# Another order of matmuls around the border batches, and four stores issued by GpSimd, in a two-layer convolution kernel

## The reference

```python
def _gn(v, G=32, eps=1e-05): ...            # per image and channel: (v - mean) / sqrt(var + eps)

x = x + _L0_conv_ref(_gn(x), w3, b3, w5, b5, wr, br)
x = x + _L1_conv_ref(_gn(x), filters)
```

```python
feat = (spot[..., :, None] * spot[..., None, :]).reshape(spot.shape[:-1] + (M * M,))
out = jnp.einsum('bcyxf,ocf->boyx', feat, filters.reshape(O, C, M * M))
```

## Time and profile before

| | |
|---|---|
| median of 3 runs | 304.87 us (304.46 to 305.16) |
| profiled execution | 305.6 us, span from first to last instruction 303.9 us |
| mean granted TensorE clock | 0.979 |
| TensorE matmul busy | 276.0 us, 91%, 6464 multiplies |
| VectorE busy | 251.5 us, 83% |
| ScalarE busy | 88.1 us, 29% |
| GpSimd busy | 33.0 us, 11% |
| DMA | 11.45 MB |

### The profile page before, as it was taken

One profiled execution on the slowest core, in us unless ns is written; L12 is line 12 of the kernel. 1 busy time (PEld: TensorE's weight loads), 2 busy tenths in 40 slices (PEclk: granted clock), 3 DMA queues, 4 the chain that ended last, 5 costly groups with the idle time before them and its releaser, 6 DMA issues.

```text
span 303.9 us, 13566 instructions
## 1 busy us (share of the span) xinstructions
PE 276.0 (91%) x6464; PEld 125.6 (41%) x6464; DVE 251.5 (83%) x216; ACT 88.1 (29%) x135; POOL 33.0 (11%) x82
## 2 busy tenths in 40 slices
PE   0579999899999999999999999999999999999930
PEld 0124443343334434436457455333334446447310
DVE  1899899995999999599999999976999999950330
ACT  5432016949258989529000000004000000000000
POOL 7913970000110000000000000000000000000000
PEclk9999999979999999999999999999999999999985
DMA  6973000000000000000000000085000000000049
GB/s 191 382 193 82 4 3 2 2 5 2 2 2 4 4 2 2 4 2 5 2 2 4 4 2 4 2 172 111 2 2 4 2 2 4 2 4 4 2 86 190
DMA packets 19206, 11.45 MB, mean 38 GB/s; under 512 B 17744, under 2 KB 17872, under 8 KB 19024
## 3 DMA queue, kind: packets, MB, share of 16 engines
q1 hardware_dynamic: 14640, 9.06, 11.7%
q10 hardware_dynamic: 4512, 1.53, 2.2%
HBM read 6.40 MB, written 4.19 MB: 35 GB/s over the span
## 4 chain that ended last, share of the span: by engine, by line
PE 80%; DVE 7%; ACT 3%; issue 3%; DMA 2%; SPq 1%; DVEq 0%
PE acc L1007 63%; PE acc L1050 15%; ACT raw L507 3%; DMA raw<-in_x 2%; DVE stats L741 2%; PE acc L1101 2%; DVE plane L759 1%; DVE raw L801 1%; DVE arena L669 1%; ACT arena L497 1%; DVE scaled L637 0%; DVE norm L756 0%; SPq L314 0%; SPq L321 0%; DVE mean_var L746 0%
## 5 line engine op out<-in xcount | busy, mean ns | idle before, releaser
L1007 PE MATMUL acc<-product,weight 32*32 32x512 f32 (+1 forms) x3040 | 128.6, 605 | 0.0
L1007 PEld LDWEIGHTS acc<-product,weight 32*32 32x32 f32 (+1 forms) x3040 | 61.7, 110 | 63.8 <-issue 51.1
L879 DVE TENSOR_TENSOR product<-plane 128x4096 f32<-128x4096 f32 x19 | 83.3, 4427 | 0.1
L1007 PE MATMUL acc<-raw,weight 32*32 32x512 f32 (+1 forms) x992 | 44.3, 605 | 0.0
L1050 PE MATMUL acc<-product,middle 32*64 32x512 f32 (+1 forms) x576 | 30.6, 621 | 0.0
L1007 PEld LDWEIGHTS acc<-raw,weight 32*32 32x32 f32 (+1 forms) x992 | 20.4, 111 | 20.7 <-issue 16.2
L801 DVE TENSOR_TENSOR raw<-acc,arena 128x512 f32<-128x512 f32 x16 | 9.9, 684 | 18.9 <-issue 18.7
L741 DVE BATCH_NORM_STATS2 stats<-raw 128x6 f32<-128x512 f32 x32 | 19.7, 686 | 3.1 <-DMA raw<-in_x 3.1
L879 DVE TENSOR_TENSOR raw<-plane 128x4096 f32<-128x4096 f32 x5 | 22.2, 4433 | 0.0
L1007 PE MATMUL acc<-product,arena 32*32 32x512 f32 (+1 forms) x448 | 22.0, 606 | 0.0
L507 ACT ACTIVATE raw<-arena 32x512 f32<-32x512 f32 x32 | 21.9, 683 | 0.5
(11 more groups left out here) (121 smaller groups left out, 213.9 us busy)
## 6 DMA issues: line engine op xcount, KB each, us to landing
raw<-in_x SPq DMA_DIRECT2D x8, 512.0 KB, 8.5
out<-raw SPq DMA_DIRECT2D x24, 128.0 KB, 2.9
arena<-in_L_conv_filters SPq DMA_DIRECT2D x4, 400.0 KB, 6.9
out<-raw ACTq DMA_DIRECT2D x8, 128.0 KB, 4.6
arena<-in_L_conv_w ACTq DMA_DIRECT2D x4, 100.0 KB, 4.0
w_in<-in_L_conv_w ACTq DMA_DIRECT2D x2, 36.0 KB, 1.9
w_in<-in_L_conv_w SPq DMA_DIRECT2D x2, 36.0 KB, 2.1
b_in<-in_L_conv_b SPq DMA_DIRECT2D x2, 0.5 KB
```

The lines of the kernel that those rows point to most:

```text
L879: nc.vector.tensor_tensor(both_halves(g, u), plane_halves(g), plane_halves(g, PRODUCTS[k][0] * PITCH + PRODUCTS[k][1]), ALU.mult)\
L1007: return nc.tensor.matmul(acc[32 * s:32 * (s + strips), j, r, :], weights[32 * r:32 * r + 32, t:t + strips, :] .rearrange("p t c -> p (t c ...
```

## The change

Group two's "total" is issued as two rounds of pairs, the border columns, two more rounds of pairs and then the round of singles; before, the singles stood between the two border batches and all four rounds of pairs behind. The rest of the first layer for group two begins with singles. In the second layer's first unit of g = 0, singles and pairs change places, so that the pairs stand between the border batches. Of group two's 16 stores, GpSimd issues strip 2 of every image with a semaphore of its own; SP issues strip 0 of every image and strip 3 of images 1 and 3, ScalarE's queue strip 1 and strip 3 of images 0 and 2.

```diff
+        stored_by_pool = sem("stored_by_pool")
...
-        def store(eng, g, r, strips):
+        def store(eng, g, r, strips, done):
...
-                              .rearrange("p (y x) -> p y x", x=W)).then_inc(stored, 16)
+                              .rearrange("p (y x) -> p y x", x=W)).then_inc(done, 16)
+
+        def store_last(eng, strips, parity, done):
+
+            for r in range(GROUP):
+                eng.wait_ge(evicted, 3 * GROUP + r + 1)
+                store(eng, 1, r, strips + ((3,) if r % 2 == parity else ()), done)
...
-                store(sp, 0, r, range(STRIPS))
-            for r in range(GROUP):
-                sp.wait_ge(evicted, 3 * GROUP + r + 1)
-                store(sp, 1, r, (0, 1))
-            sp.wait_ge(stored, 16 * NG * GROUP * STRIPS)
+                store(sp, 0, r, range(STRIPS), stored)
+            store_last(sp, (0,), 1, stored)
+            sp.wait_ge(stored, 16 * (NG * GROUP * STRIPS - GROUP))
+            sp.wait_ge(stored_by_pool, 16 * GROUP)
...
             stream_borders(raw[1]).then_inc(borders, 1)
+            store_last(pool, (2,), None, stored_by_pool)
...
-            for r in range(GROUP):
-                act.wait_ge(evicted, 3 * GROUP + r + 1)
-                store(act, 1, r, (2, 3))
+            store_last(act, (1,), 0, stored)
...
-            def column0(odd, stack, at, pitch, x0, every, five, start, stop, pairs):
+            def column0(odd, stack, at, pitch, x0, every, five, start, stop, pairs, rows):
...
                 if pairs:
-                    for d in range(-1, 3):
+                    for d in rows:
...
-            def product0(g, name, odd, start, stop, pairs):
+            def product0(g, name, odd, start, stop, pairs, rows=range(-1, 3)):
...
             edges0(0, ROW_SIDES)
-            product0(1, "total", 0, False, False, False)
+            product0(1, "total", 0, False, False, True, (-1, 0))
             edges0(0, COLUMN_SIDES)
-            product0(1, "total", 0, False, True, True).then_inc(part_done, 1)
+            product0(1, "total", 0, False, False, True, (1, 2))
+            product0(1, "total", 0, False, True, False).then_inc(part_done, 1)
             pe.wait_ge(edges_copied, 2)
-            rest0(1, PAIRS_FIRST)
+            rest0(1, SINGLES_FIRST)
...
                     for half in (0, 1):
-                        column(0, plane_pixels(0, half), every_row, sum_taps[0][:, 0:3, :], half == 0, False, PAIRS)
+                        column(0, plane_pixels(0, half), every_row, sum_taps[0][:, 0:3, :], half == 0, False, SINGLES)
                     edges0(1, ROW_SIDES)
                     for half in (0, 1):
-                        column(0, plane_pixels(0, half), every_row, sum_taps[0][:, 0:3, :], False, False, SINGLES)
+                        column(0, plane_pixels(0, half), every_row, sum_taps[0][:, 0:3, :], False, False, PAIRS)
                     edges0(1, COLUMN_SIDES)
```

More of the change, by code:

```diff
@@ L1070, in product0 @@
                     return column0(odd, plane[g], PLANE_AT - 2 * PITCH, PITCH, 2, 2, weight0[:, PAIR_AT:EDGE_AT, :],
-                                   start, stop, pairs)
+                                   start, stop, pairs, rows)
                 source, x0 = ("step", 1) if name == "step after" else (name, 0)
@@ L1077, in product0 @@
                 pe.wait_ge(middle_ready, g + 1)
-                return column0(odd, *half_at(g, source), x0, 1, five, start, stop, pairs)
+                return column0(odd, *half_at(g, source), x0, 1, five, start, stop, pairs, rows)
             def part(g, names, odd, forms):
```

## The result

The changed kernel takes 306.02 us, the median of six executions (305.58 to 306.99); the kernel before takes 304.76 in its six (303.78 to 305.16). The ratio is 1.0048, with a 95% interval of 1.0029 to 1.0068: slower, by more than the 0.2% that such a measurement can tell. The forecast was 303.0 us and faster. The size of the time stayed within the range, 301.0 to 306.5; the sign did not.

What follows compares the result with a forecast made beforehand. TensorE was taken to bound the kernel almost everywhere, with holes from missing instructions. From the 304.87 us median, minus 2.0 (first layer), minus 0.3 (second), plus 0.4 (stores) gave 303.0 us; range 301.0 to 306.5.

Steps and rivals of the forecast that it cites:

- 1.7 is the clock that does not fall: First layer, group two: of 2.3 us by which "step" starts earlier, 1.7 come from the clock staying up.
- the work that moved into the hole: First layer, between border batches: 0.6 us gained as pairs fill the idle piece of 1.54 us.
- The next instructions still arrive at 60.81: First layer, border columns: unchanged instruction count ahead keeps the packet's arrival, so the hole shrinks to 0.6 us.
- third rival: The holes belong to the borders, not to missing instructions; hole and low clock stay: 306.1 us, chance 0.07.
- first rival: First layer: the clock still falls behind a hole of 0.6 us: 304.5 us, chance 0.15.
- 0.7 off for the median: Base of the sum: the three runs' median, 304.87 us, lies 0.7 below the profiled execution.
- TensorE's arrival ahead of the border rows: First layer, group two's "total": no wait before the border rows was forecast; pairs followed them from 57.94 plus a turn.
- Second layer: Second convolution, group one: pairs between the border batches remove the hole of 0.38 us; net minus 0.3 us.
- Stores: Group two's last stores: the DMA engines are the bound, four stores on GpSimd give no bandwidth; plus 0.4 us.
- fourth rival: Stores: the issuers were the bound, so at most 2 us more are gained: 300.6 us, chance 0.10.
- the lower bound of 1.6: Stores: GpSimd's price from below, 1.6 us a store by its plain subtraction; 2.2 us was taken.
- the rival of a slow GpSimd: Stores: GpSimd builds slowly and ends later than before; 308.2 us at 3.5 us a store, chance 0.18.

Runs made afterwards that it cites:

- e5_before_again: The kernel before, unchanged, recorded for a second trace; 306.95 us, one execution.
- e8_pool8: Orders of before, eight of group two's stores on GpSimd, four each on SP and ScalarE's queue; 308.35 us, one execution.
- e1_order: The new matmul orders of both layers with the old stores, against the kernel before; 304.54 us, ratio 0.9990.
- e3_first: The new order in the first layer alone, against the kernel before; 304.48 us, ratio 0.9978.
- e12_order_again: Both new matmul orders with the old stores, run once more, against the kernel before; 304.10 us, ratio 0.9990.
- e13_race_new: New orders, old stores, GpSimd's last four filter sums held until VectorE's last half of group one, against the kernel before; 304.66 us, ratio 0.9984.
- e7_held_new: New orders, old stores, all GpSimd's filter sums held until VectorE's last half of group one, against the kernel before; 306.70 us, ratio 1.0039.
- e10_pool1: Orders of before, one of 16 stores on GpSimd (strip 2 of image 0); 304.75 us, one execution.
- e4_second: The new order in the second layer's first unit alone, against the kernel before; 305.06 us, ratio 0.9996.
- e2_stores: The new stores alone with the old matmul orders, against the kernel before; 306.00 us, ratio 1.0036.
- e11_uneven: Orders of before, no store on GpSimd, SP issuing ten of the last 16 and ScalarE's queue six; 305.12 us, one execution.

## Why the prediction was wrong, step by step

**The hole and the clock: right in the recorded execution, wrong as a price of every one.** The failed step is "1.7 is the clock that does not fall". It took one profiled execution for all. The clock fell in three of the ten recorded executions with the old order of the first layer (before, e5_before_again, e8_pool8), each time behind a hole of 1.27 us or more; it held in the seven others, and in all five with the new order. Without the fall, the old order takes 21.0 to 21.6 us from rows to x1, and the new one 21.0 to 21.7. So the order is worth some 2.3 us where the clock falls, and nothing where it does not. The forecast's other 0.6, "the work that moved into the hole", does not show either: the holes of the old order without a fall were mostly 0.71 to 1.06 us, not 1.54, and left less to fill. In the timed executions it seems rarer still. The recorded falls have a mean granted clock of 0.976 to 0.979 over the execution, those without, with stores as before, 0.984 or more. Of the 104 timed executions of before five are at 0.980 or lower, and they took 306.05 to 308.48 us. Of the 45 executions of e1_order, e3_first, e12_order_again and e13_race_new, but for the two of e1_order far off all others, none is. The six of e7_held_new stand against this: the new order with TensorE idle 2.37 us ahead of the border rows in the recorded execution. Five in a hundred at 2.3 us make 0.1 us of the mean and nothing of the median. Such a mean is a sign and no proof; how often the clock falls without a profile stays open.

**"The next instructions still arrive at 60.81": half right.** The packet follows what has been issued: it starts 1.0 to 1.5 us after the border rows with the old order and 1.1 to 1.7 after them with the new one. But the hole ended 2.9 us after the packet's start in the trace of before and 2.4 after it in that of the changed kernel. The packet itself takes from 0.88 to 1.43 us, and in all 15 traces the engine goes on 1.3 to 1.5 us after it has landed. Start and length together move the hole of one and the same order from 0.71 (e10_pool1: start at 1.0, length 0.92) to 1.54 (before: 1.25 and 1.43), and with it, it seems, the clock. The third rival, that the holes belong to the borders and not to missing instructions, is out: they shrink as the batches move apart. The Trainium skill (Runtime: NRT & Kernel Launch, Instruction fetch mechanics) has the fetch "mostly hidden"; ahead of these short matmuls it costs up to 1.54 us, so the measurement decides against it in this place. The first rival, that the clock falls all the same, did not come true in the traces: none of the holes of the new order, 0.16 to 0.55 us, brought it down. Behind a longer wait for VectorE the low means of e7_held_new leave it open.

**The base of the sum.** The forecast took 0.7 off for the median and left the parts of the recorded execution as they were. Two of them were not usual, and they nearly hid each other: the fall, 2.3 us too many, and border rows 1.0 to 1.6 us earlier than in the ten other traces without a hold, since neither GpSimd held up the half nor TensorE lost its 1.2 us before 34 us. A usual execution is then about 305.6 - 2.3 + 1.3 = 304.6 us, close to the median of 304.76. TensorE's arrival ahead of the border rows, for which I saw no wait, is a tie: in four of those ten it waits 0.3 to 1.05 us for VectorE, and in the others both arrive together.

**Second layer: right, but for one trace.** 199.98 became 199.60, 199.50 in e4_second and 199.55 and 199.69 in two others with the new order: -0.3 to -0.5, forecast -0.3. In e7_held_new it is 199.93: there a hole of 0.28 us stands in the border rows, near 95.

**Stores: right in sign, 0.4 forecast, 1.4 measured, by another mechanism.** That the engines are the bound, and not the issuers, held; the fourth rival is out. GpSimd's pace was bounded wrongly: it issues a store in 0.65 us, below the lower bound of 1.6, and its four land 1.0 to 1.6 us apart, the last at 299.95. So the rival of a slow GpSimd fell too, though its sign came true.
**The sum.** Orders -0.3, from e1_order and e12_order_again (0.999 each, with intervals that hold 1); stores +1.1 by e2_stores' ratio and +1.3 to +1.4 by the tails. Together +0.8 to +1.1. Measured were 306.02 - 304.76 = +1.26, and by the interval of the ratio 0.9 to 2.1.

## What to carry to other kernels

Before a stall in a trace is priced, take a second trace of the same kernel: a fall of the clock or a race between two engines can be one execution's and not the kernel's, and a change aimed at it gains only where it occurs. Two rare pieces can cancel and leave the median looking well explained. Here the DMA engines were the bound, and moving one, four or eight stores to a third issuer made the tail 0.2, 1.3 and 1.8 us longer: ask not how fast it issues, but when its first data move and what its packets do to the queues beside it.

## What the runs showed of the hardware that I had not expected

- GpSimd's stores of 512 pieces of 256 B are issued in 0.65 us each but begin to move 3.3 us after the issue, against 0.85 us for SP's. The Trainium skill (DMA: Bandwidth & Descriptors, Specifications) gives about 1 and 0.6 us to the first byte; for GpSimd the trace is far above that.
- A VectorE instruction of 2.29 us took 2.71 to 3.96 us beside a run of small GpSimd instructions: it lasted 2.29 us plus what was left of the whole run, less 0.13, in ten traces. In one execution GpSimd gave way instead (twelve in 10.17 us, where they take 6.04). The Trainium skill (SBUF — State Buffer, Who interferes with whom) says that an instruction of VectorE's with two inputs in SBUF contends with GpSimd's reads; the trace agrees. Holding GpSimd back by four sums took the contention away here; holding back twelve moved it to dearer work.
- The clock fell behind an idle piece of 1.27, 1.29 and 1.54 us between the thin border batches, but not behind one of 1.27 in e11_uneven, nor behind any of 1.06 or less.
- The holes between instruction packets differ from execution to execution of one order, by up to 0.8 us (0.71 to 1.54 with the old order).
